# Graph attention on one core: slot addresses packed three to a word and unpacked in registers

## What is computed

```python
messages = x[dst]                                  # 212500 edges
h = messages @ W_lin.T + b_lin
g = (messages @ W_gate.T + b_gate)[:, 0]
e = exp(g - segment_max(g, src)[src])
attn = e / (segment_sum(e, src) + 1e-16)[src]
pooled = segment_sum(attn * h, src)                # 12500 nodes, 128 features
out = layernorm(x + pooled @ W_out.T + b_out)
```

## Time and profile before

| | |
|---|---|
| median of 3 runs | 3840.32 us (3839.37 to 3845.12) |
| the profiled execution, own time | 3856.86 us |
| its span in the profile | 3855.0 us |
| TensorE matmuls busy | 1179.1 us (31%) |
| VectorE busy | 1598.2 us (41%), 5936 instructions |
| ScalarE busy | 686.8 us (18%) |
| GpSimd busy | 1645.3 us (43%) |
| granted TensorE clock, mean | 0.562 of full speed |
| DMA over the span | 143.50 MB, mean 37 GB/s |

### The profile page before, as it was taken

The page is one execution under the profiler, slowest core; times in us unless marked ns, Lnnn a source line. Parts: engine busy times, 40 slices in busy tenths (PEclk is TensorE's granted clock), DMA queues, the critical chain, the costliest instruction groups (busy, mean ns, idle before and its releaser), DMA issues.

```text
span 3855.0 us, 26980 instructions
## 1 busy us (share of the span) xinstructions
PE 1179.1 (31%) x5447; PEld 1028.6 (27%) x5447; DVE 1598.2 (41%) x5936; ACT 686.8 (18%) x2101; POOL 1645.3 (43%) x1715
## 2 busy tenths in 40 slices
PE   6221122233322332233322332223322333223352
PEld 4111122222222332222222332223222322222341
DVE  9999422243223432233323432234322432234366
ACT  3110021111211122111211112111211112111214
POOL 1100445434554355544554345544555345543505
PEclk9555555555555655555555555555555555555565
DMA  2000211111111111111111111111111111111122
GB/s 114 41 0 0 63 34 38 37 29 33 38 38 34 29 37 38 38 30 31 39 39 35 29 36 38 38 31 30 38 38 38 29 32 38 38 34 29 37 54 67
DMA packets 88552, 143.50 MB, mean 37 GB/s; under 512 B 28850, under 2 KB 60189, under 8 KB 88271
## 3 DMA queue, kind: packets, MB, share of 16 engines
q0 software_dynamic: 53152, 110.66, 12.9%
q1 hardware_dynamic: 34512, 30.91, 2.4%
q10 hardware_dynamic: 732, 0.20, 0.0%
HBM read 127.84 MB, written 13.83 MB: 37 GB/s over the span
## 4 chain that ended last, share of the span: by engine, by line
another core or an unknown queue 30%; DVE 27%; issue 26%; PE 11%; DVEq 3%; POOL 2%; ACT 1%; DMA 0%; SPq 0%; ACTq 0%; POOLq 0%
DVE nodes_sb L939 11%; PE bank L640 6%; DVE spread L934 3%; PE bank L586 2%; PE bank L620 2%; DVE rows_b L781 2%; POOL ring L405 1%; DVE rows_a L780 1%; DVE rows_a L781 1%; DVE rows_b L780 1%; DVEq L928 1%; DVE turn_b L781 1%; DVE turn_b L780 1%; DVE turn_a L781 1%
## 5 line engine op out<-in xcount | busy, mean ns | idle before, releaser
L405 POOL DMA_INDIRECT ring<-node_table,gather_at x1661 | 1570.8, 946 | 1964.2 <-ACTq L469 1470.5
L640 PE MATMUL bank<-ring,spread 128*128 x3520 | 755.6, 391 | 1866.6 <-DVE nodes_sb L939 1021.3
L934 DVE TENSOR_SCALAR spread<-iota_row,places 128x128 f32<-128x128 f32 x1760 | 498.3, 284 | 1987.5 <-remote 1241.7
L640 PEld LDWEIGHTS bank<-ring,spread 128*128 128x128 f32 x3520 | 674.5, 290 | 1943.5 <-issue 1942.6
L939 DVE SCALAR_TENSOR_TENSOR nodes_sb<-nodes_sb,drops,bank 128x129 f32 x1760 | 612.4, 348 | 3.8 <-issue 1.6
L484 ACT ACTIVATE ring<-ring,weights 128x129 f32<-128x129 f32 x1664 | 545.4, 395 | 359.5 <-issue 359.2
L467 ACT ACTIVATE gather_at<-bank 128x40 int32<-128x40 f32 x42 | 8.5, 203 | 1965.0 <-PE bank L580 1940.2
L620 PE MATMUL bank<-chosen,drop_x 40*128 40x40 f32 x352 | 82.6, 407 | 16.2 <-issue 15.4
L579 PE MATMUL bank<-ident,dst_f 40*128 40x40 f32 x42 | 12.4, 296 | 242.6 <-DVEq L724 228.1
L610 PE MATMUL bank<-chosen,row_f 40*128 40x40 f32 x352 | 83.8, 411 | 6.4 <-DVEq L747 6.4
L586 PE MATMUL bank<-ended,ones 40*128 40x40 f32 x352 | 82.9, 408 | 7.8 <-DVE ended L732 5.6
(11 more groups left out here) (150 smaller groups left out, 1047.7 us busy)
## 6 DMA issues: line engine op xcount, KB each, us to landing
ring<-node_table,gather_at POOLq DMA_INDIRECT x1661
node_table<-ring SPq DMA_DIRECT2D x1, 6347.7 KB
nodes_sb<-in_x SPq DMA_DIRECT2D x10, 625.0 KB
ring<-in_x SPq DMA_DIRECT2D x9, 448.0 KB, 5.3
out<-ring SPq DMA_DIRECT2D x9, 448.0 KB
k<-sorted_keys SPq DMA_DIRECT2D x126, 20.0 KB
rows_a<-in_x SPq DMA_DIRECT2D x2, 448.0 KB
rows_b<-in_x SPq DMA_DIRECT2D x2, 448.0 KB
```

The lines of the kernel that those rows point to most:

```text
L405: pool.indirect_dma_start(out=chunk_rows[c % RING][:, t, :], out_offset=None, in_=table[:, :], in_offset=bass.IndirectOffsetOnAxis(ap=gath ...
L640: last = pe.matmul(tile_ps(slot), lhsT=spread[:, slot, :], rhs=ring[:, bass.ds(got[slot], WIDTH)], start=True, stop=True)
L934: return dve.tensor_scalar(spread[:, slot, :], iota_row[:, :], places[n % 2][:, t:t + 1], None, ALU.is_equal)
```

## The change

Each engine's address numbers are packed three to a 24-bit word, eight bits each: the number of a block (0 to 97) for VectorE, the number of a tile's place in the ring (0 to 199) for TensorE. A round of 40 slots takes 14 words. There are two loads a round on each engine: before b = 0 (six words, slots 0 to 15) and before b = 4 (nine words, slots 16 to 39). The loads before b = 2, 6 and 8 are gone. Every use of a number is now an expression on a loaded word: shift right by 0, 8 or 16, mask with 255, times 129 (VectorE) or 130 (TensorE). `place_slots` packs: it keeps the numbers unscaled, and makes each word in two steps of multiply by 256 and add, with a drain between them. In place of the one instruction of line 750 there are four small ones and one more drain on 1 partition and 14 elements.

```diff
+PACK, PACK_BITS = 3, 8
+WORDS = -(-T // PACK)
+LOADS = {0: (0, 16), 4: (15, T)}
...
+        slot_cols, slot_blocks = sb("slot_cols", [1, PACK * WORDS]), sb("slot_blocks", [1, PACK * WORDS])
+        packed = sb("packed", [1, 2, WORDS])
...
-        dve_at = [sb(f"dve_at{k}", [1, T], I32) for k in range(2)]
-        pe_at = [sb(f"pe_at{k}", [1, T], I32) for k in range(2)]
+        dve_at = [sb(f"dve_at{k}", [1, WORDS], I32) for k in range(2)]
+        pe_at = [sb(f"pe_at{k}", [1, WORDS], I32) for k in range(2)]
...
+        def unpacked(table, b, engine):
+
+            first, end = LOADS[b]
+            got = nc.values_load_multi_w_load_instructions(
+                table[0:1, first // PACK:-(-end // PACK)], engines=[engine], min_val=0, max_val=(1 << PACK * PACK_BITS) - 1,
+                skip_runtime_bounds_check_because="three numbers of eight bits")[1]
+            return {t: got[t // PACK - first // PACK] >> t % PACK * PACK_BITS & (1 << PACK_BITS) - 1
+                    for t in range(b * BATCH, end)}
...
             def sum_slots(n):
+                at = {}
...
-                    if b % 2 == 0:
+                    if b in LOADS:
                         pe.nop(nofuse=True)
-                        many = min(2, batches_of(n) - b) * BATCH
-                        got = nc.values_load_multi_w_load_instructions(
-                            pe_at[n % 2][0:1, b * BATCH:b * BATCH + many], engines=[mybir.EngineType.PE], min_val=0,
-                            max_val=(RING * T - 1) * ROW, skip_runtime_bounds_check_because="a tile's place in the ring")[1]
+                        at.update(unpacked(pe_at[n % 2], b, ENGINE.PE))
                     for u in range(BATCH):
                         slot = (b % 2) * BATCH + u
-                        last = pe.matmul(tile_ps(slot), lhsT=spread[:, slot, :], rhs=ring[:, bass.ds(got[slot], WIDTH)],
+                        place = nc.s_assert_within(at[b * BATCH + u], 0, RING * T - 1, skip_runtime_bounds_check_because="a tile's place in the ring")
+                        last = pe.matmul(tile_ps(slot), lhsT=spread[:, slot, :], rhs=ring[:, bass.ds(place * ROW, WIDTH)],
                                          start=True, stop=True)
...
-            dve.tensor_scalar(base_cols[:, :], iota_row[0:1, 0:T], float((WINDOW - 1) * T), float(WIDTH), ALU.add, ALU.mult)
+            dve.tensor_scalar(base_cols[:, :], iota_row[0:1, 0:T], float((WINDOW - 1) * T), None, ALU.add)
+            dve.memset(slot_cols[:, :], 0.0)
+            dve.memset(slot_blocks[:, :], 0.0)
...
-                dve.scalar_tensor_tensor(dve_at[n % 2][:, :], at[0:1, :], float(-WIDTH), base_cols[:, :], ALU.mult, ALU.add)
+                dve.scalar_tensor_tensor(slot_blocks[:, 0:T], at[0:1, :], -1.0, base_cols[:, :], ALU.mult, ALU.add)
...
-                dve.scalar_tensor_tensor(slot_cols[:, :], wraps[:, :], float(-RING * T), place[:, :], ALU.mult, ALU.add)
+                dve.scalar_tensor_tensor(slot_cols[:, 0:T], wraps[:, :], float(-RING * T), place[:, :], ALU.mult, ALU.add)
                 dve.drain()
-                dve.tensor_scalar(pe_at[n % 2][:, :], slot_cols[:, :], float(ROW), None, ALU.mult)
+                thirds = [v[:, :].rearrange("p (w k) -> p k w", k=PACK) for v in (slot_blocks, slot_cols)]
+                for k in range(2):
+                    dve.scalar_tensor_tensor(packed[:, k, :], thirds[k][:, 2, :], float(1 << PACK_BITS), thirds[k][:, 1, :], ALU.mult, ALU.add)
+                dve.drain()
+                for k, into in enumerate((dve_at, pe_at)):
+                    dve.scalar_tensor_tensor(into[n % 2][:, :], packed[:, k, :], float(1 << PACK_BITS), thirds[k][:, 0, :], ALU.mult, ALU.add)
...
             def slot_values(n, b):
-                many = min(2, batches_of(n) - b) * BATCH
...
+                return unpacked(dve_at[n % 2], b, ENGINE.DVE)
...
             def add_slot(n, t, slot, at_col):
-                here = sums[:, bass.ds(at_col, WIDTH)]
+                here = sums[:, bass.ds(nc.s_assert_within(at_col, 0, BLOCKS - 1, skip_runtime_bounds_check_because="a block's number") * WIDTH, WIDTH)]
                 dve.wait_ge(sums_added, slots_upto(n) + t + 2 * BATCH)
...
             def spread_batch(n, b, at, adds=None):
-                if b % 2 == 0:
+                if b in LOADS:
                     dve.nop(nofuse=True)
```

More of the change, by code:

```diff
@@ L87, in check_shapes @@
     assert BLOCKS % GB == 0 and GROUPS % 2 == 0
+    assert max(RING * T, BLOCKS) <= 1 << PACK_BITS and PACK * PACK_BITS <= 24 and SLOTS > (ROUNDS - 1) * T + T - BATCH
 def tiles_of(c):
@@ L183, in graph_attention @@
         slot_rows = [sb(f"slot_rows{k}", [P, T]) for k in range(2)]
-        slot_cols = sb("slot_cols", [1, T])
+        slot_cols, slot_blocks = sb("slot_cols", [1, PACK * WORDS]), sb("slot_blocks", [1, PACK * WORDS])
+        packed = sb("packed", [1, 2, WORDS])
         window_at = sb("window_at", [T, WINDOW, WINDOW])
@@ L926, in slot_values @@
             def slot_values(n, b):
-                many = min(2, batches_of(n) - b) * BATCH
-                got = nc.values_load_multi_w_load_instructions(
-                    dve_at[n % 2][0:1, b * BATCH:b * BATCH + many], engines=[mybir.EngineType.DVE],
-                    min_val=0, max_val=(BLOCKS - 1) * WIDTH, skip_runtime_bounds_check_because="a block times the width")[1]
-                return {b * BATCH + k: got[k] for k in range(many)}
+                return unpacked(dve_at[n % 2], b, ENGINE.DVE)
             def spread_slot(n, t, slot):
```

## The result

The changed kernel takes **4211.4 us** (median of 4 runs, 4206.8 to 4212.5), the kernel before 3839.9 beside it (median of 4): a ratio of 1.096, 95% interval 1.095 to 1.098, so 371 us slower. The forecast was 3954 with a range of 3830 to 4005: the direction was right, the time far outside.

A forecast was written before the change was run, and what follows sets the result against it. The prediction took the nine VectorE batches after the last gather to bound each round. Unpacking 3.2 plus TensorE 0.1 minus loads saved 0.7 gave +2.6 us a round, +114 us over 44 rounds: 3954 us, range 3830 to 4005.

The forecast's parts named there:

- What bounds the kernel: Each round of 79.7 us: 50 us of gathers, about 4.4 us, nine VectorE batches, about 4 us; batches 0 to 2 hidden.
- free stretch: Nine VectorE batches, from batch 3 after the last gather to the next `prepare`; on the path, 21.56 or 19.69 us a round.
- Load time by words: Rival: the nine-word load before batch 4 costs 0.075 us more on either engine, 0.15 a round, 3961 us; chance 0.05.
- Nine words are two loads: Rival: a second load on VectorE, then TensorE, ahead of batch 4 adds 1.2 us a round, 4007 us; chance 0.08.
- Instructions of their own: In each slot's address work, shift and mask are separate register operations, 1.65 a slot and engine, taken at 70 ns each.
- Behind the wait: In `add_slot` the address operations follow the wait for the add before, so their time adds to the 0.48 us step.
- Rival 1: Unpacking is free on VectorE, ahead of the wait or under 15 ns an operation; only loads count, 3809 us; chance 0.14.
- 70 ns on 28 slots: On VectorE after the gathers, 28 of 36 slots pay 1.65 operations of 70 ns each: 3.2 us a round.
- TensorE's 0.1 us: TensorE's added operations hide behind its products, except at the first slot of batch 4: 0.1 us a round.
- Loads saved: Dropping the loads before batches 2, 6 and 8 gains 0.55 to 0.9 us a round, taken as 0.7.
- "Hidden" beside the gathers: Whatever batches 0 to 2 gain or lose while gathers run, and the 0.7 us of packing in `place_slots`, costs nothing.
- What would show it: Signs: 88 loads, adds every 0.59 us, 23 to 24 us from batch 3 to `prepare`, no idle before batch 8.

The follow-up runs named there:

- long-round sessions: Sessions, several kernels run in turn on one chip, in which the kernel before takes 3840 to 3897 us and a round 79 us or more.
- short-round session: A session in which the kernel before, with the same instructions, takes 2671 to 2677 us, a round takes 50.1 us, and all ten batches run while GpSimd gathers.
- kernel with the nine-word loads: The kernel before, nothing to unpack, but the load ahead of batch 4 takes nine words from word 5 on both engines: 4002.8 us against 3854.9, ratio 1.0389.
- second comparison: The changed kernel again, unaltered, beside the kernel before: 4226.4 us for 3895.5, ratio 1.0847.
- kernel with aligned loads: The changed kernel with its two loads begun at words 0 and 8, eight words each: ratios 1.0052 to 1.0057 to the kernel before, measured only with 50.1 us rounds.

## Why the prediction was wrong

**What bounds the kernel: right** for long-round sessions. The round follows the free stretch, 7.1 of the 8.1 us. But I took the creep of batches 0 to 2 as a property of the kernel, and it is one of the session: in six of ten sessions it was absent, and there the change's parts cost 0.4 to 0.7%. No row of one trace could have shown that.

**"Load time by words": the step that failed.** I priced the nine-word load at 0.075 us more than the eight-word one, 0.15 a round, by dividing 0.596 by eight, and left it as a rival with a chance of 0.05. It measured 1.48 + 1.59 us of load and 3.25 us of free stretch a round: 148 us in the run that has nothing else. My mean divided by eight words what the chip loaded as two aligned fours, and no row had a load of another size or start, so there was nothing to scale from. "Nine words are two loads" (4007 us, 0.08) had the right place and the right path, VectorE's load and then TensorE's, with 1.2 us a round for 3.3; the range should have held its worse forms. The Trainium skill (Runtime: NRT & Kernel Launch, Instruction fetch mechanics) gives about 200 ns a register even in bulk, for the runtime's own register loads from HBM; ours come from SBUF. I let the row of eight words overrule it. The single words here take 0.22 to 0.23 us each, so its figure is near the trace where a load doesn't begin at a multiple of four, and far above it for aligned fours (0.25 us for four). By it the nine-word load would have been 1.8 us, the six-word one 1.2 (estimates); they measured 2.07 and 0.80.

**"Instructions of their own": right**, 2904 records on each engine, 66 for 40 slots.

**"Behind the wait": right, and it decides.** Moving the wait, and nothing else, took the free stretch from 24.05 to 19.76 us in a short-round session; with the loads mended as well the kernel took 0.9999 of the one before in a long-round one. Rival 1, free unpacking, described that kernel's registers and not this one's, but its gain of 31 us did not come there either.

**70 ns on 28 slots: the price was near, the number of slots too small.** Two operations lengthen the step from 0.48 to 0.64 us and one to 0.56. 11 ns of that are the longer address record, which I hadn't foreseen; the rest is 72 to 76 ns an operation. But I had called the first slot of batches 3 to 6 covered, and it is so only in part: against the kernel with the nine-word loads its add comes 0.07 to 0.10 us later after its `spread`, the other adds 0.14 to 0.15 each (means over rounds 1 to 39). The slots of the eight batches outside batch 5 cost 4.2 us a round, 3.2 was forecast. (My own count was off too: the four first slots and batch 5's four share one, so they leave 29.) Batch 5 was covered, as I had said. The same two traces, both of long-round sessions, show it: batch 5's slots take 0.5 us longer, step b5-b6 only 0.19, and the mean idle ahead of batch 6 falls from 2.66 to 2.35 us.

**TensorE's 0.1 us: 0.19.** That is the growth of b5-b6: from the VectorE work that releases TensorE to its first product of batch 4 it takes 2.78 us for 2.59. Its products hide the other operations at a granted clock of 0.50, where four of them take 2.08 us with or without unpacking. At 1.00 they don't: 1.40 us for 1.15 in batch 6. And I had no term for the clock itself, which stayed at 0.50 in batches 7 and 8. It cost little, since little waits for TensorE there: 0.2 us a round ahead of batch 9. Whether the slower rhythm of the products keeps the clock down was not tested.

**Loads saved: 0.7 forecast, about right.** The gap ahead of batch 8 is 0.73 us shorter than in the kernel with the nine-word loads; from five to two loads in short-round sessions it was 1.0 (25.1 to 24.1 us).

**The sum of a round, all from long-round traces.** Long loads 3.25 us (the nine-word kernel less the one before: 23.43 - 20.18). Then the change less the nine-word kernel, 27.29 - 23.43 = 3.86: the slots of nine batches 4.65, less 0.30 that falls into the wait ahead of batch 6, less 0.73 for the load ahead of batch 8, plus 0.20 ahead of batch 9, plus 0.04 around the next batches 0 and 1, where the six-word load stands. Together 7.11, as measured; 2.6 was forecast, with nothing for the long loads, 3.3 for the rest of what was added and 0.7 for the loads saved. The three traces come from two sessions, whose kernels before differ by 15 us in all.

**"Hidden" beside the gathers: not quite in the first comparison.** Batches 0 to 2 and what stands around them were to cost nothing. There the time from the gathers' end to batch 3 grew by 0.94 us a round, 41 us in all; the second comparison, of 331 us, leaves at most 17 us for it, with the free stretch and the part after the last gather taken as in the first (7.11 x 40 + 29.8 = 314).

**What would show it.** 88 loads, the idle ahead of batch 8 gone (its mean fell from 0.66 us to nothing), waits beside the gathers within 1 us (+0.94): as written. Adds at 0.59: 0.61 in the mean of 26 slots at 0.64 and 14 at 0.56. A free stretch of 23 to 24 us: that is what the kernel with aligned loads has (24.05). The long loads are what this line missed.

## What to carry to other kernels

Cut a register load so that it begins at a multiple of four words, and fill it up to whole fours with words nobody needs: seven words from word 0 took 1.04 us and eight took 0.61, and the nine of this change, cut at word 5, took 2.07. Hang a wait on the instruction that needs it, and not on one of its own ahead of address arithmetic: 4.3 us of a round's free stretch went that way (24.05 to 19.76), with one instruction fewer for each add. Whether it pays is another matter: the kernel before, which has little address work, was 0.2% slower with it where the gathers are the bound. And a time per item, worked out from one size, says nothing of a size beyond it, nor of another starting point.

## What the runs showed that I had not expected

- **Register loads**: 0.1 us, plus 0.25 for each four words of a load that begins at a multiple of four, plus 0.2 to 0.25 for each other word, in the 27 of 30 shapes that fit.
- **The same kernel at 3840 and at 2672 us.** In short-round sessions the page has no idle of `spread` put down to a remote queue; GpSimd's gathers follow each other all through. The waits of the kernel before in that trace (2669.7 us span), where the gathers' only idle is the 0.3 us between them and the one wait at the start:

```profile
POOL ring L406 <- issue: 505.9, 1660, 0.3
...
DVE spread L936 <- PE bank L641: 364.7, 213, 5.9
...
POOL ring L406 <- ACTq L470: 282.1, 1, 282.1
```

  What holds batches 0 to 2 in the other condition, and what makes a session one or the other, is open: no experiment was aimed at it. In the short-round condition the gathers should cover all that the change adds but the 29.8 us after the last gather (an estimate from its long-round trace; the change itself was not had there). The aligned-loads kernel bears it out: 13 to 16 us slower in all, 15 to 16 after the last gather. So a comparison made in one condition alone would mislead.
- **Faster batches, slower gathers.** Where gathers are the bound, the two kernels with VectorE's adds closer together had gathers of 50.1 us a round for 49.8 and a total 0.2 to 0.3% longer, though the stretch after the last gather became 3 to 5 us shorter (112.3 to 109.2 and 107.0 us).
